# Counting sort with its counts scanned one chunk ahead, and row sums with five buffer sets

## The reference, cut to what matters

```
z   = segment_sum(x[src] * edge_weight, ...)            # layer 0
h   = relu(bn(relu(bn(cat(x[row], x[col]) @ W1)) @ W2)) # layer 1, summed by row
for (W, b) in ((W1, b1), (W2, b2)):                     # layer 2, twice
    h = h @ W
    agg = segment_sum(h[src] * norm, dst)
    h = agg + h * inv_deg + b
for _ in range(6):                                      # layer 3
    msg = einsum('ei,eio->eo', out[src], w_e)
    h = gru(relu(segment_sum(msg, dst) + conv_bias), h)
```

## Time and profile before

| what | us |
|---|---|
| median of 3 runs | 42493.79 (42493.11 to 42507.26) |
| the profiled execution's own time | 42484.64 |
| its span | 42482.9 |

### The profile page before, as it was taken

How to read it: one execution, slowest core, us unless ns; L and a number is a source line. 1 busy time by engine, 2 the same in 40 slices (tenths; PEclk the granted TensorE clock), 3 DMA queues, 4 the chain that set the end, 5 groups by cost and what they waited for, 6 DMA issues and landing times. The chain is left out here.

```text
span 42482.9 us, 515512 instructions
## 1 busy us (share of the span) xinstructions
PE 30089.3 (71%) x99425; PEld 18060.8 (43%) x99426; DVE 29028.6 (68%) x63440; ACT 11309.4 (27%) x26426; POOL 30959.9 (73%) x31499
## 2 busy tenths in 40 slices
PE   5222234444465222259999999999999999999999
PEld 5332323333364222234444444444444444444444
DVE  7333322221164222259999999999999999999999
ACT  0000001111120000014444444444444444444444
POOL 1665655555513666669998998899899989998997
PEclk8555556655565555569999999999999999999999
DMA  1110012221131010011111111111111111111111
GB/s 45 41 41 24 20 33 62 60 38 21 21 80 22 12 11 13 12 26 46 45 46 44 46 45 44 46 45 46 43 45 46 45 43 46 45 46 43 45 46 42
DMA packets 1365773, 1669.95 MB, mean 39 GB/s; under 512 B 847197, under 2 KB 1012048, under 8 KB 1252304
## 3 DMA queue, kind: packets, MB, share of 16 engines
q1 hardware_dynamic: 664232, 1115.69, 7.9%
q0 software_dynamic: 669696, 495.09, 7.8%
q10 hardware_dynamic: 31680, 57.69, 0.4%
HBM read 1393.98 MB, written 274.47 MB: 39 GB/s over the span
## 5 line engine op out<-in xcount | busy, mean ns | idle before, releaser
L1723 PE MATMUL l3m_p_w<-en,l3m_hid 128*128 128x512 f32 x42240 | 20968.2, 619 | 650.6 <-issue 272.0
L1773 DVE TENSOR_REDUCE l3m_xg<-l3m_prod 128x32 f32<-128x1024 f32 x10560 | 12849.9, 1217 | 188.6
L1645 POOL DMA_INDIRECT l3m_xg<-wide_table,l3m_mt x10560 | 10340.8, 979 | 2413.5 <-issue 2161.2
L1654 POOL TENSOR_TENSOR l3m_prod<-l3m_rest,l3m_xg 128x384 f32<-128x384 f32 x10560 | 10674.1, 1011 | 280.0 <-ACT l3m_rest L1700 93.6
L1723 PEld LDWEIGHTS l3m_p_w<-en,l3m_hid 128*128 128x128 f32 x42240 | 7165.9, 189 | 6865.7 <-issue 5382.0
L1700 ACT COPY l3m_rest<-l3m_p_w 128x384 f32<-128x384 f32 x10560 | 5050.4, 478 | 12801.7 <-PE l3m_p_w L1723 11891.0
L1785 DVE TENSOR_TENSOR l3m_prod<-l3m_p_w,l3m_xg 128x512 f32<-128x512 f32 x10560 | 7186.1, 681 | 423.4 <-PE l3m_p_w L1723 235.2
L1735 PEld LDWEIGHTS l3m_p_sum<-l3m_xg,l3m_apart 128*125 128x125 f32 x21120 | 3965.7, 188 | 5090.1 <-issue 2742.7
L1688 ACT ACTIVATE l3m_apart<-iota_lo,l3m_mt 128x125 f32<-128x125 f32 x10560 | 4239.1, 402 | 14.4 <-issue 13.4
L1735 PE MATMUL l3m_p_sum<-l3m_xg,l3m_apart 128*125 128x64 f32 x21120 | 3474.7, 246 | 22.3 <-DVE l3m_xg L1773 22.3
L858 POOL DMA_INDIRECT l2a_xg<-table,l2a_mt x1760 | 1677.0, 953 | 2220.7 <-DMA l2a_mt<-dst_meta 1673.6
(11 more groups left out here) (328 smaller groups left out, 22330.7 us busy)
## 6 DMA issues: line engine op xcount, KB each, us to landing
l3m_hid<-hid_t SPq DMA_DIRECT2D x660, 1024.0 KB
l3m_xg<-wide_table,l3m_mt POOLq DMA_INDIRECT x10560
hid_t<-l_hid SPq DMA_DIRECT2D x110, 1024.0 KB, 4.1
order_src_bk<-dst_bucket SPq DMA_DIRECT2D x52, 808.0 KB
order_dst_bk<-src_bucket SPq DMA_DIRECT2D x52, 808.0 KB
by_dst<-order_src_empty SPq DMA_DIRECT2D x28, 1071.0 KB
l_rec<-by_dst SPq DMA_DIRECT2D x110, 272.0 KB, 3.7
l_xg<-table,l_mt POOLq DMA_INDIRECT x1760
```

Of the source, the lines that this page charges most:

```text
L1645: pool.indirect_dma_start(xg[s][:, j, 0:2 * D], None, wide_table[:, :], bass.IndirectOffsetOnAxis(ap=mt[s][:, j, 0:1].bitcast(I32), axis=0 ...
L1654: pool.tensor_tensor(o_i(prod[j % RING][:, OWN:HD]), o_i(rest[j % RING][:, :]), state_of(s, j, REST), ALU.mult).then_inc(pooled, 1)
L1723: ins = pe.matmul(p_w[j % 2][:, c * 512:(c + 1) * 512], hid[s][:, j * P:(j + 1) * P], en2[:, c * 512:(c + 1) * 512], start=True, stop=True)
L1773: dve.tensor_reduce(xg[s][:, j, 2 * D:3 * D], o_i(prod[j % RING][:, :]), AX, ALU.add).then_inc(msgs, 1)
```

## The change

In the sort, DVE's stream is split into `scan` (compare, prefix sums, `count`) and `place` (row numbers to `idx`), and its order becomes scan(c+1), place(c), scan(c+2), place(c+1). `count` and `p_pos` get two buffers each. SP's order becomes keys(c+1), records(c), keys(c+2), records(c+1). PE's loop covers two chunks. For the two sums of layer 2 a new function `sum_rows` takes the place of `gather_sum`, with five buffer sets; SP fetches metadata when the hits are found and the rows have landed (it does not wait for PE), and DVE finds hits four groups ahead of the adds. The 16 adds and 16 finds of a group and the 16 gathers are the same instructions as before. `add_sums` gets the number of buffer sets as an argument; its other callers are unchanged. `sum_rows` ends with 14 semaphores to clear, `gather_sum` with 8.

```
-                count = ph.sb("count", [P, CHUNK])
+                count = [ph.sb(f"count{s}", [P, CHUNK]) for s in range(2)]
-                p_pos = ph.ps("p_pos", [P, 512])
+                p_pos = [ph.ps(f"p_pos{s}", [P, 512]) for s in range(2)]
...
+                        keys(0, 0)
+                        with sp.Fori(0, NCH // 2 - 1) as i:
+                            keys(i, 1)
+                            records(i, 0)
+                            keys(i + 1, 0)
+                            records(i, 1)
+                        keys(NCH // 2 - 1, 1)
+                        records(NCH // 2 - 1, 0)
+                        records(NCH // 2 - 1, 1)
...
+                        def place(i, s):
+                            c = i * 2 + s
+                            dve.wait_ge(ranked, c + 1)
+                            dve.tensor_scalar(pos[:, :], p_pos[s][:, 0:CC], -1.0, None, ALU.add)
...
+                            dve.wait_ge(free, c + 1)
+                            dve.scalar_tensor_tensor(out=idx[s][:, :], ...).then_inc(indexed, 1)
+
+                        scan(0, 0)
+                        with dve.Fori(0, NCH // 2 - 1) as i:
+                            scan(i, 1)
+                            place(i, 0)
+                            scan(i + 1, 0)
+                            place(i, 1)
+                        scan(NCH // 2 - 1, 1)
+                        place(NCH // 2 - 1, 0)
+                        dve.drain()
+                        place(NCH // 2 - 1, 1)
...
-                        with pe.Fori(0, NCH) as c:
-                            pe.wait_ge(placed, c + 1)
+                        with pe.Fori(0, NCH // 2) as i:
+                            for s in range(2):
+                                pe.wait_ge(placed, i * 2 + (s + 1))
...
+        NBUF = max(n for n in range(2, 6) if NG % n == 0)
+
+        def sum_rows(tag, meta, tab, off, acc):
...
+                        for s in range(NBUF):
+                            fetch(0, s)
+                        with sp.Fori(0, NG // NBUF - 1) as i:
+                            for s in range(NBUF):
+                                sp.wait_ge(hits, i * NBUF + (s + 1))
+                                sp.wait_ge(rows_in[s], i * (16 * G) + 16 * G)
+                                sp.sem_inc(begun, 1)
+                                fetch(i + 1, s)
...
+                        with pool.Fori(0, NG // NBUF) as i:
+                            for s in range(NBUF):
+                                pool.wait_ge(meta_in[s], i * 16 + 16)
+                                pool.wait_ge(summed, i * NBUF + (s + 1))
+                                pool.sem_inc(begun, 1)
+                                for j in range(G):
+                                    pool.indirect_dma_start(...).then_inc(rows_in[s], 16)
...
+                        dve.sem_inc(added, NBUF * G)
+                        for s in range(NBUF - 1):
+                            find(0, s)
+                        with dve.Fori(0, NG // NBUF - 1) as i:
+                            for s in range(NBUF):
+                                if s:
+                                    find(i + 1, s - 1)
+                                else:
+                                    find(i, NBUF - 1)
+                                add(i, s)
+                        find(NG // NBUF - 1, NBUF - 1)
+                        for s in range(NBUF):
+                            add(NG // NBUF - 1, s)
...
+                        pe.sem_inc(summed, NBUF)
+                        with pe.Fori(0, NG // NBUF) as i:
+                            for s in range(NBUF):
+                                pe.wait_ge(hits, i * NBUF + (s + 1))
+                                pe.wait_ge(rows_in[s], i * (16 * G) + 16 * G)
+                                pe.wait_ge(added, (i * NBUF + s) * G + G)
...
-        gather_sum("l2a", dst_meta, 2, table, False, off_d, ACC)
+        sum_rows("l2a", dst_meta, table, off_d, ACC)
-        gather_sum("l2b", dst_meta, 2, table, False, off_d, ACC)
+        sum_rows("l2b", dst_meta, table, off_d, ACC)
```

More of the change, by code:

```diff
@@ L397, in _ @@
                             sp.dma_start(recs[:, f * FILL:(f + 1) * FILL, :], empty[:, :, :]).then_inc(filled, 16)
[L398 to L416, removed]
@@ new lines, in keys, with records @@
+                        def keys(i, s):
+                            c = i * 2 + s
+                            sp.wait_ge(keys_free, c + 1)
+                            sp.sem_inc(begun, 1)
+                            sp.dma_start(bk[s][0:K, :],
+                                         chunk(bucket_d, c)[None, :].broadcast_to([K, CHUNK])).then_inc(keys_in[s], 16)
+                        def records(i, s):
+                            c = i * 2 + s
+                            sp.wait_ge(free, c + 1)
+                            sp.sem_inc(begun, 1)
+                            for to, of in ((far[s], a[other]), (lot[s], lo_d)):
+                                sp.dma_start(to[:, :], chunk(of, c).rearrange("(p t) -> p t", t=CC)).then_inc(rec_in[s], 16)
+                            if R == SR:
+                                of = chunk(a["edge_weight"], c).rearrange("(p t) -> p t", t=CC)
+                                sp.dma_start(wgt[s][:, :], of).then_inc(rec_in[s], 16)
+                            else:
+                                of = a["edge_attr_32"][bass.ds(c * CHUNK, CHUNK), :].rearrange("(p t) f -> p t f", t=CC)
+                                sp.dma_start(rec[s][:, :, 2:R], of).then_inc(rec_in[s], 16)
@@ L428, in _ @@
                         dve.tensor_copy(carry[:, :], start[:, :]).then_inc(keys_free, 2)
[L429 to L434, removed]
-                                dve.drain()
[L437 to L460, removed]
@@ new lines, in place @@
+                        def place(i, s):
+                            c = i * 2 + s
+                            dve.wait_ge(ranked, c + 1)
+                            dve.tensor_scalar(pos[:, :], p_pos[s][:, 0:CC], -1.0, None, ALU.add)
+                            dve.drain()
+                            dve.tensor_scalar(row[:, :], pos[:, :], P - 1, None, ALU.bitwise_and)
+                            dve.tensor_scalar(pos[:, :], pos[:, :], 7, None, ALU.arith_shift_right)
+                            dve.drain()
+                            dve.wait_ge(free, c + 1)
+                            dve.scalar_tensor_tensor(out=idx[s][:, :], in0=row[:, :], scalar=float(TT),
+                                                     in1=pos[:, :], op0=ALU.mult, op1=ALU.add).then_inc(indexed, 1)
```

70 lines of the change are left out of this document (62 added, 8 removed).

## The result

The changed kernel takes 43298.94 us (median of 4 runs, 43287.15 to 43299.83); the kernel before took 42500.53 beside it. The ratio is 1.0186, 95% interval 1.017 to 1.0202. I forecast 42240 and a range up to 42680: it is slower by 800 us, and outside.

What follows compares the result with a forecast made beforehand. POOL's indirect DMAs bound the four changed stages, pausing while PE catches up; 87 + 90 + 21 + 63 - 6 - 2 = 253 us off 42484.6 gave 42232, so 42240 for the runs, range 41600 to 42680.

Steps and rivals of the forecast that it cites:

- Most of that is layer 3, the last 24 ms, which the change leaves alone: Opening step: most of POOL's busy time, 73% of the span, lies in layer 3, taken as untouched by the change.
- the slower one: Rival for layer 2's sums: POOL pauses at every group of 16 DMAs, +160 us per sum, 42820 us; chance 0.15.
- -87 and -90: Layer 2's first and second sum: gains of 87 and 90 us, from pauses of 427.6 and 430.0 us.
- 5.6 to 7.1: All four stages: pause in us still needed per 32 POOL DMAs for PE to catch up, however many buffers; 6.3 taken.
- the sort chunk's 64 records: Sort, PE: about 11 of 64 records delivered while POOL sent, the other 53 in 6.5 us after its stop.
- the pair's 64: Sums, PE's pair of groups: 8.4 of the first 32 records by POOL's stop, the remaining 55.6 in 8.6 us.
- 8.2 and 6.5 records per us: PE's assumed delivery rates with POOL still, in the sort chunk and the sums, against 0.45 while POOL sends.
- the chain behind PE's release: Waits that go: metadata fetch and landing in the sums, 2.6 us; row numbers in the sorts, about 1.7 us, partly.
- 1 us, for the semaphores: Ends of layer 2's two sums: 12 more semaphores to clear cost 2 us in all (0 to 5).
- -21 and -63: First and second sort: gains of 21 and 63 us, from pauses of 342.5 and 383.8 us.
- no measurable change: Rival: POOL's bursts and pauses both lengthen, one sort pause per two chunks, 42400 to 42580 us; chance 0.15.
- the bad case named there: Sort starts: 3.2 us later each, but up to a scan more (17 us) if the second key load is late.

Runs made afterwards that it cites:

- `PLACE = 160`: The changed kernel with 160 instead of 32 VectorE drains ahead of layer 3's outer loop: 43305.4 us, ratio 1.0181 to the kernel before.
- `PLACE = 96`: The kernel before with 96 instead of 32 VectorE drains ahead of layer 3's outer loop: 43228.64 us, ratio 1.0163.
- two sets: The changed kernel with two buffer sets instead of five in `sum_rows` and no drains ahead of layer 3's loop: first sum 2545.8 us.
- `PLACE = 0`: The changed kernel without the 32 VectorE drains ahead of layer 3's outer loop: 42280.89 us, ratio 0.9941 to the kernel before.

## Why the prediction was wrong

- "Most of that is layer 3, the last 24 ms, which the change leaves alone": the step that failed. The source of layer 3 is left alone, its place in VectorE's instruction stream is not. Shown from both sides: the changed kernel is cured by 32 drains fewer, the kernel before is spoiled by 64 more. The loss, 1057 us, exceeds every term of the sum. It came in although VectorE had 2.9 us of slack per iteration, because the stop is longer than that. The clues stood in the material: `PLACE = 32` in the source, a loop of 301 instructions, and the q14 row. None of my rivals had it; the slower one put 160 us into each sum.
- The Trainium skill has the rule, in "Runtime: NRT & Kernel Launch", section "Instruction fetch mechanics": most engines' store is 32 KiB, 512 instructions, and a taken branch whose target has left it forces a fetch. The trace agrees in kind: three fetches stand at the branch. In size it doesn't: 512 instructions are four blocks of 128, and a loop of 301 instructions that touches four is fetched anew. The Trainium skill gives the block there as 16 KiB; here VectorE's packets are 8192 bytes, and with blocks of 256 `PLACE = 160` would have been fast and so would `PLACE = 96` in the kernel before. Both were slow.
- The sums: -87 and -90 forecast, -126 and -127 measured. The pauses came to 5.9 us per 32 DMAs, inside 5.6 to 7.1. But the cause was wrong, so this agreement is luck. PE's records are not what a pause supplies (half of them: 304 against 308 us). The earlier trace rows spoke against it already: of the sort chunk's 64 records, 53 stand before POOL's stop and 11 behind it, where I had put 11 and 53, and 32 of the pair's 64 are done at 14512.48, where I had 8.4. My 8.2 and 6.5 records per us are also faster than PE itself (64 in 14.03 us, 4.6 per us). What the term for the chain behind PE's release priced was real: the fetch off that chain alone won 106 us (two sets). I had taken a symptom, PE's and VectorE's instructions coming singly, 1.4 to 2.8 us apart, while POOL sends, for the cause.
- Behind each sum I had 1 us, for the semaphores; it is +28, which five sets bring: with two sets the gap is 91.7 us instead of 124.6. With five, PE and VectorE can be several groups in arrears when POOL ends.
- The sorts: -21 and -63 forecast, -43 and -51 measured, with 26 and 34 pauses for 51, each longer, as the rival "no measurable change" has it. (That rival's 39 records left at the stop don't follow from its 2.2 us each: 64 less 18 are 46.) The starts were the bad case named there: 18 and 17 us instead of 3 each. Alone, the sorts' part is 1.0006.
- "POOL runs through" had 0.10. It is what happens in a condition without pauses, and by its time with the kernel before just as well.

What stays open: what the backlog is, why some whole runs don't have it, and the +12 us between the second sort and layer 2 (they lie in gathers of unchanged code, which differ by as much from run to run: layer 1's takes 2946 us before, 2951 after, 2960 with `PLACE = 0`). A floor near 1.40 us per DMA fits the kernels above that have pauses; it wasn't tried where it could have failed.

## What to carry to other kernels

Before a change that adds code to an engine, count the instructions of its longest loops, and where they start: a loop near the size of the instruction store can be lost by code far ahead of it, and the row of the instruction queue shows it at once. Try each part alone, but also the sum of their lengths. If a stall follows an engine's burst, halve the suspect's work first: a reading that gives the right size may still name the wrong cause.

## What the runs showed that I had not expected

- Instruction fetches that repeat stop VectorE for 4.7 to 5.7 us per iteration of a loop of 301 instructions (0.7 us without them). Of that 2.39 to 3.38 us are lost where it had 2.9 us of slack, and nothing where it has more. Each stop also costs PE its full clock for the next 6.8 us.
- While POOL sends indirect DMAs, single instructions of PE and VectorE come mostly 1.4, 2.1 or 2.8 us apart, and for some 5 us behind its stop. In the changed kernel's first sum POOL stops at 14325.68, and PE and VectorE are at pace from about 14331:

```profile
14323.18 0.21 PE L900 MATMUL l2a_p_sum<-l2a_xg,l2a_hit 128*125 128x32 f32 x1 [2.59 <-issue]
14324.60 0.28 PEld L900 LDWEIGHTS l2a_p_sum<-l2a_xg,l2a_hit 128*125 128x125 f32 x1 [2.54 <-issue]
...
14326.00 0.21 PE L900 MATMUL l2a_p_sum<-l2a_xg,l2a_hit 128*125 128x32 f32 x1 [2.61 <-issue]
14327.40 0.28 PEld L900 LDWEIGHTS l2a_p_sum<-l2a_xg,l2a_hit 128*125 128x125 f32 x1 [2.52 <-issue]
...
14331.76 0.94 POOL L858 DMA_INDIRECT l2a_xg<-table,l2a_mt  x1 [6.08 <-remote]
```

- This holds in most comparisons and in two not at all: the kernel before takes 42289 to 42529 us with it and 39623 to 39634 without, one chip having shown both.
- A drain of POOL behind an indirect DMA holds the next one up by 1.8 us (2.13 us of idle time for 0.30) to 2.7 (3.02, behind 16). In the run with one behind 16, a drain's record ends at 13921.4, 0.5 us after the rows' landing let PE go (13920.98), so it seems to wait for the landing.
